# Down projection of four of eight passes computed token by feature, with the output bias added on GpSimd

## The reference

```python
x = x + 0.5 * ffn(layernorm(x), gate_w, w1, b1, w2, b2)     # first half
x = x + mixer(layernorm(x), ...)                            # norm, conv, gates, scan, head mix, out projection
x = x + 0.5 * ffn(layernorm(x), gate_w, w1, b1, w2, b2)     # second half, same weights

# ffn, per sequence: the mean token is routed to 2 of 8 experts, weights softmaxed over the two
hmid = gelu(einsum('bth,hf->btf', x, w1[e]) + b1[e])        # 128 -> 512
y    = einsum('btf,fh->bth', hmid, w2[e]) + b2[e]           # 512 -> 128
out += combine[:, e] * y
```

## Time and profile before

| | us |
|---|---|
| median of 3 runs | 269.35 (269.06 to 269.4) |
| the profiled execution | 268.6 |
| its span, first to last instruction | 266.8 |
| TensorE matmul busy | 253.0 (95%) |
| VectorE busy | 225.8 (85%) |
| ScalarE busy | 213.5 (80%) |
| GpSimd busy | 53.6 (20%) |
| mean granted TensorE clock | 0.996 |

### The profile page before, as it was taken

How to read it: one execution, slowest core, us unless ns; L and a number is a source line. 1 busy time by engine, 2 the same in 40 slices (tenths; PEclk the granted TensorE clock), 3 DMA queues, 4 the chain that set the end, 5 groups by cost and what they waited for, 6 DMA issues and landing times.

```text
span 266.8 us, 3674 instructions
## 1 busy us (share of the span) xinstructions
PE 253.0 (95%) x1060; PEld 177.8 (67%) x1060; DVE 225.8 (85%) x561; ACT 213.5 (80%) x260; POOL 53.6 (20%) x69
## 2 busy tenths in 40 slices
PE   7569999999999989999999999999999999999993
PEld 7348785565665746665666666658868688887881
DVE  3679978896899999999899999999999999655462
ACT  1379897567999937997957999789999997989862
...
PEclk9999999999999999999999999999999999999998
...
GB/s 185 171 244 336 93 81 157 158 217 242 17 0 0 2 0 207 31 1 2 0 143 96 0 2 129 107 0 2 2 14 223 0 2 0 129 266 3 0 4 154
DMA packets 16596, 22.83 MB, mean 86 GB/s; under 512 B 1152, under 2 KB 11648, under 8 KB 16576
## 3 DMA queue, kind: packets, MB, share of 16 engines
...
q10 hardware_dynamic: 688, 0.27, 0.4%
...
...
## 4 chain that ended last, share of the span: by engine, by line
PE 81%; DVE 5%; ACT 5%; issue 3%; DMA 2%; POOL 1%; SPq 1%; DVEq 0%; ACTq 0%; POOLq 0%
PE y_ps L790 35%; PE hid_ps L758 29%; PE aux_ps L861 5%; PE aux_ps L814 4%; PE aux_ps L893 3%; PE aux_ps L842 2%; PE aux_ps L882 2%; DMA w_sb<-wpack_dram 1%; DMA xt<-x_dram 1%; DVE xc L1129 1%; DVE late L1229 1%; POOL f_rstd L409 1%; ACT late L645 1%; DVE xt L1098 1%; DVE late L1237 0%
## 5 line engine op out<-in xcount | busy, mean ns | idle before, releaser
L758 PE MATMUL hid_ps<-z_hi,w_parts 128*128 128x512 f32 x256 | 89.8, 433 | 2.1 <-ACT w_parts L518 1.5
L556 ACT ACTIVATE hid<-hid_ps,w_sb 128x1024 f32<-128x1024 f32 x64 | 70.8, 1110 | 8.4 <-PE hid_ps L758 7.2
L790 PE MATMUL y_ps<-hid,w_sb 128*128 128x512 f32 x144 | 68.4, 597 | 0.3
L758 PEld LDWEIGHTS hid_ps<-z_hi,w_parts 128*128 128x128 f32 x256 | 47.3, 188 | 21.8 <-issue 10.9
L1078 DVE TENSOR_TENSOR hid_lo<-hid,hid_hi 128x1024 fp32r<-128x1024 f32 x28 | 34.0, 1221 | 11.1 <-ACT hid_hi L563 11.0
L790 PEld LDWEIGHTS y_ps<-hid,w_sb 128*128 128x128 f32 x144 | 25.9, 189 | 21.5 <-issue 19.3
L758 PE MATMUL hid_ps<-z_lo,w_parts 128*128 128x512 f32 x128 | 39.9, 393 | 0.0
L563 ACT ACTIVATE hid_hi<-hid 128x1024 fp32r<-128x1024 f32 x28 | 29.5, 1058 | 3.1 <-PE y_ps L790 2.7
L758 PEld LDWEIGHTS hid_ps<-z_lo,w_parts 128*128 128x128 f32 x128 | 24.0, 188 | 5.7
L407 POOL TENSOR_SCALAR f_ve<-f_mv 128x8 f32<-128x8 f32 (+1 forms) x9 | 3.0, 337 | 108.0 <-DVE f_mv L957 108.0
L790 PE MATMUL y_ps<-hid_hi,w_hi 128*128 128x512 f32 x56 | 18.3, 408 | 1.2 <-DVE w_lo L1070 1.1
...
## 6 DMA issues: line engine op xcount, KB each, us to landing
...
w_sb<-wpack_dram SPq DMA_DIRECT2D x16, 258.5 KB, 3.8
...
```

The lines of the kernel that those rows point to most:

```text
L556: nc.scalar.activation(hid[:, slot % HBUF, :], hid_ps[:, slot % 2, :], ACT.Gelu, bias=bias).then_inc(hid_ready, 1)
L758: last = nc.tensor.matmul(hid_ps[:, slot % 2, cols], w, z[:, q % 2, cols], start=first, stop=end)
L790: last = nc.tensor.matmul(y_ps[:, cols], wt, src[:, cols], start=t == 0 and i == 0, stop=t == SLOTS - 1 and end)
```

## The change

Passes 1 to 4 (TOKEN_PASSES) compute the down product token by feature: 128 tokens of `hid` are the stationary operand and a 128x128 block of w2 the moving one, 8 matmuls a slot. `y_ps` then has the layout of `xt`. `pass_out` and `post` are left out for these passes; `update_x` multiplies `y_ps` by `coef` and adds it to `xt`, in two halves, the first of which may start when the first four tiles of the last slot are through. The first down slot of the following pass waits for these updates. The output bias, now along the free axis, is loaded as 128 equal rows (`wpack` has 128 more columns, and the w2 loads of these passes are longer); GpSimd's `token_bias` weighs and adds the rows of the two experts and adds the result to `xt`, after the pass's normalise step has read it. `out_bias` falls away for these passes. Several waits are added or renumbered, and nearly all places in AT are new.

```diff
+TOKEN_PASSES = (1, 2, 3, 4)
 AT = {
     "pe": {
-        "f_norm": {1: 166, 2: 306, 3: 749, 4: 1089, 5: 1449, 6: 1806, 7: 2126},
-        "f_route": {1: 229, 2: 449, 3: 926, 4: 1249, 5: 1489, 6: 1829, 7: 2166},
-        "m_norm": {0: 509, 1: 849, 2: 1189, 3: 1569},
-        "m_dt": {0: 649, 1: 949, 2: 1309, 3: 1706},
-        "m_v": {0: 669, 1: 989, 2: 1349, 3: 1746},
-        "m_gate": {0: 889, 1: 1229, 2: 1609, 3: 1966},
-        "m_heads": {0: 909, 1: 1269, 2: 1649, 3: 2013},
-        "m_out": {0: 932, 1: 1289, 2: 1693, 3: 2026},
-        "y_turn_y": {0: 409, 1: 729, 2: 1069, 3: 1429, 4: 1860, 5: 2046, 6: 2592, 7: 2692},
+        "f_norm": {1: 166, 2: 306, 3: 789, 4: 1129, 5: 1469, 6: 1806, 7: 2166},
+        "f_route": {1: 206, 2: 409, 3: 889, 4: 1189, 5: 1509, 6: 1829, 7: 2186},
+        "m_norm": {0: 549, 1: 849, 2: 1149, 3: 1489},
+        "m_dt": {0: 709, 1: 1029, 2: 1349, 3: 1706},
+        "m_v": {0: 729, 1: 1069, 2: 1389, 3: 1726},
+        "m_gate": {0: 809, 1: 1209, 2: 1529, 3: 1926},
+        "m_heads": {0: 929, 1: 1309, 2: 1669, 3: 2044},
+        "m_out": {0: 949, 1: 1329, 2: 1693, 3: 2048},
+        "y_turn_y": {0: 429, 5: 2206, 6: 2592, 7: 2692},
     },
     "dve": {
-        "f_stats": {1: 81, 2: 207, 3: 400, 4: 959, 5: 1312, 6: 1712, 7: 2053},
-        "f_scale_w2": {0: 140, 1: 531, 2: 808, 3: 1073, 4: 1333, 5: 1649, 6: 2008, 7: 2343},
-        "f_bias": {0: 396, 1: 667, 2: 982, 3: 1111, 4: 1337, 5: 1688, 6: 2160, 7: 2322},
-        "m_stats": {0: 433, 1: 750, 2: 1090, 3: 1454},
-        "m_normalise": {0: 496, 1: 830, 2: 1173, 3: 1544},
-        "m_silu_lo": {0: 648, 1: 947, 2: 1305, 3: 1691},
-        "m_gated": {0: 924, 1: 1281, 2: 1669, 3: 2019},
-        "m_add": {0: 939, 1: 1296, 2: 1701, 3: 2039},
-        "y_update": {0: 421, 1: 740, 2: 1077, 3: 1441, 4: 1943, 5: 2077, 6: 2601, 7: 2657},
+        "f_stats": {1: 72, 2: 212, 3: 381, 4: 996, 5: 1345, 6: 1711, 7: 2095},
+        "f_scale_w2": {0: 140, 1: 556, 2: 725, 3: 1136, 4: 1530, 5: 1741, 6: 2048, 7: 2366},
+        "f_bias": {0: 209, 5: 2055, 6: 2282, 7: 2321},
+        "m_stats": {0: 453, 1: 729, 2: 1041, 3: 1375},
+        "m_normalise": {0: 529, 1: 830, 2: 1139, 3: 1475},
+        "m_silu_lo": {0: 699, 1: 1016, 2: 1330, 3: 1692},
+        "m_gated": {0: 941, 1: 1322, 2: 1683, 3: 2057},
+        "m_add": {0: 966, 1: 1337, 2: 1702, 3: 2070},
+        "y_update": {0: 437, 1: 709, 2: 1026, 3: 1363, 4: 1730, 5: 2382, 6: 2601, 7: 2657},
     },
     "act": {
-        "y_out": {0: 368, 1: 693, 2: 1013, 3: 1312, 4: 1670, 5: 1993, 6: 2310, 7: 2640},
+        "y_out": {0: 370, 5: 1993, 6: 2310, 7: 2640},
     },
     "pool": {
-        "m_rms": {0: 459, 1: 773, 2: 1113, 3: 1477},
-        "m_affine": {0: 747, 1: 997, 2: 1427, 3: 1912},
+        "f_rstd": {1: 40, 2: 174, 3: 534, 4: 952, 5: 1390, 6: 1560, 7: 1977},
+        "f_bias": {1: 427, 2: 722, 3: 1331, 4: 1362},
+        "m_rms": {0: 482, 1: 751, 2: 1061, 3: 1411},
+        "m_affine": {0: 554, 1: 942, 2: 1306, 3: 1954},
+        "m_carry": {0: 821, 1: 1110, 2: 1475, 3: 1749},
     },
     "sp": {
-        "f_load": {1: 315, 2: 567, 3: 939, 4: 1262, 5: 1510, 6: 1856, 7: 2195},
+        "f_load": {1: 245, 2: 536, 3: 934, 4: 1226, 5: 1560, 6: 1886, 7: 2211},
     },
...
@@ load_experts (SyncE)
-                    sp.wait_ge(bias2_ready, q - 1)
+                    if in_tokens(q - 2):
+                        sp.wait_ge(bias_added, token_passes(q - 1))
+                    else:
+                        sp.wait_ge(bias2_ready, turned_passes(q - 1))
...
-                    sp.dma_start(w_sb[:, q % 2, k, :],
-                                 wpack[bass.ds(e, 1), :, F:].rearrange("e p n -> p (e n)")).then_inc(w2_in[q % 2][k], 16)
+                    size = PACK - F if in_tokens(q) else B2_ROWS
+                    sp.dma_start(w_sb[:, q % 2, k, 0:size],
+                                 wpack[bass.ds(e, 1), :, F:F + size].rearrange("e p n -> p (e n)")).then_inc(w2_in[q % 2][k], 16)
@@ GpSimd
+            def token_bias(q):
+                for k in range(TOP):
+                    pool.wait_ge(w2_in[q % 2][k], 16 * (q // 2 + 1))
+                pool.wait_ge(coef_ready, TOP * (q + 1))
+                i = token_passes(q)
+                if i:
+                    pool.wait_ge(bias_added, i)
+                for k in range(TOP):
+                    nc.gpsimd.tensor_scalar(bias_tok[:, k, :], w_sb[:, q % 2, k, B2_ROWS:B2_ROWS + D],
+                                            coef[:, q % 2, k:k + 1], None, ALU.mult).then_inc(bias_step, 1)
+                pool.wait_ge(bias_step, 3 * i + 2)
+                nc.gpsimd.tensor_tensor(bias_tok[:, 0, :], bias_tok[:, 0, :], bias_tok[:, 1, :],
+                                        ALU.add).then_inc(bias_step, 1)
+                pool.wait_ge(bias_step, 3 * i + 3)
+                pool.wait_ge(f_norm_done, NT * (q + 1))
+                xb = xt[:, q % B, :, :]
+                nc.gpsimd.tensor_tensor(xb, xb, bias_tok[:, 0, :].unsqueeze(1).broadcast_to([P, NT, D]),
+                                        ALU.add).then_inc(bias_added, 1)
@@ top_tanh (ScalarE)
+                if q:
+                    act.wait_ge(coef_ready, TOP * q)
@@ down (TensorE)
-                if t == 0 and q:
-                    pe.wait_ge(yt_ready, q)
+                if t == 0 and q and not in_tokens(q - 1):
+                    pe.wait_ge(yt_ready, turned_passes(q))
+                if in_tokens(q):
+                    pe.wait_ge(hid_ready, slot + 1)
+                    for i in range(NT):
+                        if t == 0 and in_tokens(q - 1) and i % (NT // 2) == 0:
+                            pe.wait_ge(x_updated, 2 * q - 1 + i // (NT // 2))
+                        cols = slice(i * P, (i + 1) * P)
+                        last = nc.tensor.matmul(y_ps[:, cols], hid[:, slot % HBUF, cols],
+                                                w_sb[:, q % 2, k, W2_AT + f * P:W2_AT + (f + 1) * P],
+                                                start=t == 0 and i % (NT // 2) == 0,
+                                                stop=t == SLOTS - 1 and i % (NT // 2) == NT // 2 - 1)
+                        if t == SLOTS - 1 and i == NT // 2 - 1:
+                            last.then_inc(y_head_done, 1)
+                    last.then_inc(hid_used, 1)
+                    return
...
+                        if t == 0 and i == 0 and q and in_tokens(q - 1):
+                            pe.wait_ge(x_updated, 2 * q - 1 + half)
@@ pass_stats, coefficients, mixer_stats, mixer_times_dt (VectorE)
-                    dve.wait_ge(f_rstd_done, q)
+                    dve.wait_ge(f_norm_done, NT * q)
...
+                if q >= 2 and in_tokens(q - 2):
+                    dve.wait_ge(x_updated, 2 * (q - 1))
+                elif q >= 2:
+                    dve.wait_ge(yt_ready, turned_passes(q - 1))
...
+                    dve.wait_ge(m_norm_done, NT * b)
...
+                if b:
+                    dve.wait_ge(final_done, b)
@@ update_x (VectorE)
+                    if in_tokens(q):
+                        dve.wait_ge(bias_added, token_passes(q + 1))
+                        if half == 0:
+                            dve.wait_ge(y_head_done, token_passes(q + 1))
+                        else:
+                            dve.wait_ge(hid_used, SLOTS * (q + 1))
+                        V.scalar_tensor_tensor(xb[:, cols], y_ps[:, cols], coef[:, q % 2, 0:1], xb[:, cols],
+                                               ALU.mult, ALU.add).then_inc(x_updated, 1)
+                        continue
```

More of the change, by code:

```diff
@@ new lines @@
+        "m_clip": {0: 586, 1: 886, 2: 1179, 3: 1514},
[3 rows of a table added]
+        "m_silu": {0: 677, 1: 982, 2: 1314, 3: 1660},
+        "m_silu_lo": {0: 699, 1: 1016, 2: 1330, 3: 1692},
+        "m_decay": {0: 747, 1: 1078, 2: 1394, 3: 1813},
+        "m_cos": {0: 778, 1: 1115, 2: 1452, 3: 1793},
+        "m_sin": {0: 792, 1: 1127, 2: 1464, 3: 1901},
+        "m_dstep": {0: 803, 1: 1156, 2: 1495, 3: 1836},
+        "m_carry": {0: 819, 1: 1200, 2: 1533, 3: 1918},
+        "m_u": {0: 820, 1: 1186, 2: 1520, 3: 1931},
@@ new lines @@
+        "f_logits": {1: 213, 2: 385, 3: 866, 4: 1180, 5: 1493, 6: 1820, 7: 2146},
+        "f_split_w1": {1: 293},
+        "f_tanh": {1: 390, 2: 395, 3: 933, 4: 1300, 5: 1580, 6: 1890, 7: 2153},
+        "m_scale": {0: 540, 1: 830, 2: 1146, 3: 1466},
+        "m_tap": {0: 580, 1: 853, 2: 1170, 3: 1506},
+        "m_silu": {0: 620, 1: 946, 2: 1260, 3: 1626},
+        "m_silu_hi": {0: 660, 1: 980, 2: 1270, 3: 1670},
+        "m_dt": {0: 700, 1: 1020, 2: 1340, 3: 1700},
+        "m_swap": {0: 740, 1: 1060, 2: 1380, 3: 1710},
@@ L151, in macaron_kernel @@
     POOL_STEPS = 4
-    assert D == P and N == 2 * HALF and PACK == 2 * F + FT + 1
+    assert D == P and N == 2 * HALF and PACK == 2 * F + FT + 1 + D
     H = vecs.shape[1] - 4 - 3
@@ L278, in macaron_kernel @@
```

(14 more changed lines are left out.)

93 lines of the change are left out of this document (38 added, 55 removed), and 6 rows, old and new, of the table AT.

## The result

The changed kernel takes **267.72 us** (median of 5 runs, 267.48 to 268.62) against 269.35 (269.06 to 270.39) beside it: ratio 0.9945, 95% interval 0.9923 to 0.9966. Timed again as the base of the experiments it takes 267.80 against 269.11, ratio 0.9956 (0.9943 to 0.9969). So it is faster, by 1.3 to 1.6 us; the prediction said 3.2.

The account below looks back on a forecast made before the run. TensorE bounds the kernel (81% of the chain), VectorE nearly full: -1.6 (TensorE's sum) - 2.3 (stalls) + 0.4 (hand-over) + 0.3 (bias) = -3.2 us, so 266.1 us from 269.35, range 263.6 to 270.0.

Parts of the forecast that it names:

- TensorE's sum: Passes 1 to 4: 32 down slots cost +1.9 us, four `post` calls fall away for -3.5, together -1.6 us.
- GpSimd's bias: GpSimd's add onto x in passes 1 to 4: mostly covered, +0.3 us booked, 0 to 5.
- the new places: Moved fillers on TensorE's path: three quarters of 2.96 us of stalls regained, -2.3 us, bounds 0 and -4.3.
- hand-over of `y_ps`: First down slot of the next pass waits for VectorE's update of x: +0.4 us after passes 3 and 4, 0 to 1.5.
- The stalls of rows 5: Five TensorE waits between 53 and 100 us, for m_tok, silu_lo, yt, gated product and logits: 2.96 us, -2.3 expected.
- VectorE's -1.7: `out_bias` leaves VectorE's queue in four passes, eight small steps of 0.22 us: -1.7 us of VectorE's work.
- Loads: Longer w_sb loads and added waits: 0; only pass 7's load lacks cover, 6.6 us against 6.3, up to 0.6.
- B: Rival: the stalls only move, leaving TensorE's sum alone, 267.2 to 268.8 us, centre 267.7; chance 0.19.
- D: Rival: GpSimd starves at `token_bias(3)` before `update_x(3)`, or `mixer_rms(3)` behind `token_bias(4)`; slower, 271.5 us; chance 0.12.
- C: Rival: new waits after passes 3 and 4 and pass 7's load eat the gain, 268.8 to 269.9 us; chance 0.12.
- E: Rival: weight loads of the short down-slot pieces aren't hidden, about 310 us, or 274 at 2.02 a slot; chance 0.02.
- what would make the prediction wrong: Signs against it: a down slot over 1.85 us, or, last, VectorE's operations growing beside the GpSimd add.

Follow-up runs that it names:

- carry3_early: The changed kernel with VectorE's cumulative decay of m_carry(3) at place 1837 instead of 1918: 265.52 us.
- coef4_early: The changed kernel with VectorE's coefficients of pass 4 at place 1344 instead of 1359: 266.06 us.
- three_moves: The changed kernel with coefficients of pass 2 at 706, of pass 4 at 1344, and m_carry(3) of VectorE at 1837: 264.24 us.

## Why the prediction was right or wrong

The forecast was -3.2 us; at the same clock it was -1.4. Term by term: TensorE's sum -1.6 against -1.6, GpSimd's bias +2.0 against +0.3, and all that is left, the new places with the hand-over of `y_ps`, -1.8 against -1.9. So the step that made the number wrong is the bias, from the sentence "GpSimd yields, VectorE doesn't". The -1.8 came out by luck: more was regained than forecast, and a wait that wasn't in the prediction took the surplus.

- **Down slots and posts, -1.6 on TensorE: right.** 1.78 us a slot, loads of 192 ns hidden, 32 transposes fewer. One sign failed: TensorE's busy time rose, from 253.0 to 255.3 us. The half clock explains it: between 10 and 20 us alone it was busy 8.53 us against 6.20. In `carry3_early`, which kept the full clock and has one edit more, it is 250.6.
- **The stalls of rows 5, -2.3: too small.** All five are gone, and with the small gaps the table gives -4.7 up to 136 us, beyond the bound of -4.3. (The first of the five was read too long: 2.04 is the length of eight transposes by their records, which is 1.04 for undisturbed ones, so the stall was 1.0 and not 1.17.)
- **The new places can't be worse than 0: the reason was wrong, though the net stayed inside the bounds.** That term looked only at stalls which the moves take away. A move also shifts steps against each other: `m_carry(3)`, at 1918 instead of 1854, came later, while the queue that waits for it came earlier. Price: 2.0 us. The kernel before held the sign of it: line 454 at 2.22 us is the second of these very steps, waiting in the same way, and I read it as a price for the add alone.
- **GpSimd's bias, +0.3 (0 to 5): mis-sized; it measured 2.0.** The add's own length was near (2.4 us against the estimate of 2.0), and it was never stretched in the changed kernel. What failed is the sentence "GpSimd yields, VectorE doesn't". It rested on hid_lo at 1.26 beside line 454, where VectorE had come first. Where GpSimd comes first, VectorE waits: 2.26 instead of 0.68, and 4.64 instead of 2.14. The Trainium skill says so (SBUF — State Buffer, Who interferes with whom): `tensor_scalar`, which these products are, can take the pair of ports that VectorE shares with GpSimd; whoever issues first has it for the whole instruction, and the other blocks. These rows agree in time; which ports an operation used they don't show. The rule on the order has one exception here: line 494 began ahead of VectorE's lines 1251 and 1038 and still went behind them (3.49 us). The prediction had taken half of a sentence: the Trainium skill (GPSIMD Engine Reference, Key points) names instructions of VectorE in a 2-port perf mode beside those with two SBUF inputs, and only the second kind was looked for.
- **VectorE's -1.7: gone.** `out_bias` fell away, but the products at line 1222 took 2.1 us more, and the update from `y_ps` 0.74 us a half instead of 0.68.
- **Hand-over of y_ps, +0.4: it cost nothing.** No wait of the first down slots for x shows; the one of 0.43 us stands in `coef4_early` and `three_moves`.
- **Loads, 0: right.** No wait of TensorE for w_sb or w_parts in the passes; the load of pass 7 had 6.8 us and fitted.
- **The rivals.** 267.7 is B's centre to the digit, but by chance: the stalls didn't move along, they went, and as much was lost by other causes. D's second place is near what happened: not `mixer_rms(3)` but the rstd of pass 5, which stands between it and `token_bias(4)`, came late, at 1.4 us instead of the several that made D slower; its first place, before the update of pass 3, never cost anything. C and E didn't show. And of "what would make the prediction wrong" it was the last item: VectorE's operations grew beside the add.

It took both causes. Without the add the kernel takes 265.77 us, with `m_carry(3)` moved 265.52, and the forecast was 265.0 to 267.2.

Open: some 0.8 us lost between 136 and 176 us, and 0.7 us between 203 and 234 us, remain in the best kernel. The wait of 0.43 us for x, at 144.16 us, is part of the first; the rest wasn't traced.
